# A four-layer graph network on one core: new item orders on all engines and new PSUM banks

## The reference

```python
x = LN(x + attention(x, adj))     # 8 heads; softmax/3 + adj/3 + exp(-adj)/3 as weights, W_out
x = LN(x + hypergraph(x, adj))    # h = LN(relu(Dn*(H B H^T x W1) + b1)); y = Dn*(H B H^T h W2) + b2 + x
x = LN(x + diffusion(x, adj))     # T = adj*exp(leaky(sj+si)) / row sum; relu(x Wk0 + T x Wk1 + T T x Wk2)
x = LN(x + mean_aggregate(x, adj))# relu([x, adj x / deg] W3)
```

## Time and profile before

| | us |
|---|---|
| median of 3 runs (lowest, highest) | 1391.9 (1388.77, 1392.45) |
| profiled execution, its own time | 1394.77 |
| span of the profiled execution | 1393.0 |
| PE busy | 1319.9 (95%) |
| PEld busy | 1132.3 (81%) |
| DVE busy | 1162.7 (83%) |
| ACT busy | 899.1 (65%) |
| POOL busy | 623.1 (45%) |
| TensorE's mean granted clock | 0.982 |

### The profile page before, as it was taken

One profiled execution on the slowest core, in us unless ns is written; L12 is line 12 of the kernel. 1 busy time (PEld: TensorE's weight loads), 2 busy tenths in 40 slices (PEclk: granted clock), 3 DMA queues, 4 the chain that ended last, 5 costly groups with the idle time before them and its releaser, 6 DMA issues.

```text
span 1393.0 us, 32474 instructions
## 1 busy us (share of the span) xinstructions
PE 1319.9 (95%) x9705; PEld 1132.3 (81%) x9705; DVE 1162.7 (83%) x3449; ACT 899.1 (65%) x2677; POOL 623.1 (45%) x1094
## 2 busy tenths in 40 slices
PE   4799999999999999999999999999999999999975
PEld 4688888888888888888888888888888888888863
DVE  2588888888888889888888888888988888888873
ACT  3466666667666666766666766666676666676641
POOL 3135444345554345545434454443554543445442
PEclk8899999999999999999999999999999999999996
DMA  5000000000000000000000000000000000000000
GB/s 186 14 14 21 20 11 16 12 20 20 20 11 16 12 20 20 20 20 11 16 12 20 20 20 19 12 13 15 20 20 20 11 16 12 20 20 20 9 8 8
DMA packets 35588, 28.32 MB, mean 20 GB/s; under 512 B 7664, under 2 KB 34416, under 8 KB 35568
## 3 DMA queue, kind: packets, MB, share of 16 engines
q1 hardware_dynamic: 33984, 27.27, 6.2%
q0 software_dynamic: 176, 0.52, 0.2%
q10 hardware_dynamic: 1408, 0.27, 0.1%
HBM read 19.67 MB, written 8.39 MB: 20 GB/s over the span
## 4 chain that ended last, share of the span: by engine, by line
issue 35%; POOL 24%; DVE 20%; PE 13%; ACT 2%; POOLq 1%; DVEq 1%; ACTq 0%
POOL rs L1441 9%; DVE prob L1124 7%; POOL rs L1439 4%; POOL resid L1478 3%; POOL resid L1480 3%; PE PS L405 3%; DVE neg_max L1115 3%; PE PS L401 2%; PE PS L402 2%; POOL xout L1496 2%; PE PS L526 2%; ACT yT_hi L914 2%; POOL gate L1464 2%; POOL yT_lo L1509 1%; DVE xT_lo L1057 1%
## 5 line engine op out<-in xcount | busy, mean ns | idle before, releaser
L1439 POOL TENSOR_TENSOR rs<-mv,eps_c 128x1 f32<-128x1 f32 (+1 forms) x288 | 60.2, 209 | 343.8 <-DVE mv L1065 343.7
L1124 DVE SCALAR_TENSOR_TENSOR prob<-prob,rl,gate 128x128 f32<-128x128 f32 x512 | 199.7, 450 | 6.6 <-DVE rl L1121 0.4
L833 ACT ACTIVATE prob<-PS,neg_max 128x128 f32<-128x128 f32 x512 | 180.1, 381 | 3.0 <-DVE neg_max L1115 1.8
L1441 POOL TENSOR_TENSOR rs<-rs,mhalf 128x1 f32<-128x1 f32 (+1 forms) x288 | 165.5, 575 | 22.6
L816 ACT ACTIVATE qk<-PS 128x512 f32<-128x512 f32 x128 | 76.5, 599 | 120.5 <-PE PS L479 120.4
L475 PE MATMUL PS<-xT_hi,wqk_hi 128*128 128x256 f32 x512 | 137.9, 290 | 6.4 <-DVE wk_lo L1050 4.3
L476 PE MATMUL PS<-xT_hi,wqk_lo 128*128 128x256 f32 x512 | 134.2, 284 | 0.0
L1505 POOL TENSOR_TENSOR z<-z,bk_bc 128x256 f32<-128x256 f32 x64 | 48.7, 780 | 188.5 <-ACT z L892 188.5
L833 ACT ACTIVATION_READ_ACCUMULATOR prob<-PS,neg_max 128x1 f32 x512 | 113.0, 221 | 0.0
L475 PEld LDWEIGHTS PS<-xT_hi,wqk_hi 128*128 128x128 f32 x512 | 98.4, 192 | 13.9 <-issue 11.5
L479 PE MATMUL PS<-xT_lo,wqk_hi 128*128 128x256 f32 x512 | 103.1, 283 | 0.0
(11 more groups left out here) (215 smaller groups left out, 4383.7 us busy)
## 6 DMA issues: line engine op xcount, KB each, us to landing
xin<-in_x_dram SPq DMA_DIRECT2D x32, 256.0 KB, 2.7
out_dram<-xout SPq DMA_DIRECT2D x32, 256.0 KB, 2.2
...
```

The costliest lines, as they stand in the source:

```text
L833: last = act.activation(prob[:, t, h, :], PS[:, bank, k * P:(k + 1) * P], ACT.Exp, bias=neg_max[:, t, h:h + 1], accum_out=row_sum[:, t, h: ...
L1124: last = dve.scalar_tensor_tensor(prob[:, t, h, :], prob[:, t, h, :], rl[:, t, h:h + 1], gate[:, t], ALU.mult, ALU.add)
L1439: step.done(pool.tensor_tensor(rs[:, n, gs, 0], mv[:, n, gs, 1], eps_c[:].to_broadcast([P, graphs]), ALU.add))
L1441: return pool.tensor_tensor(rs[:, n, gs, 1], rs[:, n, gs, 0], mhalf[:].to_broadcast([P, graphs]), ALU.pow)
```

## The change

The orders of the items in `group` are new on TensorE, ACT, DVE and POOL. All but a few PSUM banks are new, and with them the places where an `after` holds an item back. In the set-up, the first transposes and projections of group 0 on TensorE (`xT0_(0)`, `adjT_(0)`, `qk_(0, 0)`, `qk_(0, 1)`), which were a call of `group`, are written out in a fixed order with a wait behind each. No operation is added or taken away.

The banks of the table, three of its lines:

```diff
-        bank_qk = (4, 5, 3, 6)
+        bank_qk = (1, 1, 3, 6)
...
-        bank_si = (3, 4)
+        bank_si = (3, 3)
...
-        bank_T2 = (3, 1)
+        bank_T2 = (5, 6)
```

TensorE, the set-up and the group:

```diff
-                group(None, None, 0)
-
+                xT0_(0)
+                pe.wait_ge(act_xT0, 1)
+                pe.wait_ge(dve_xT0, 1)
+                adjT_(0)
                 pe.wait_ge(act_adjT, 1)
+                qk_(0, 0)
+                pe.wait_ge(act_qk, 1)
+                qk_(0, 1)
                 pe.wait_ge(act_qk, 2)
-                pe.wait_ge(dve_xT0, 1)
                 pe.wait_ge(set_beta, 2)
...
                 if F:
                     qk_(i, 2)
                 if B:
+                    after(pe, dve_o3, 2, s - 2, 1)
                     h_(j, 0)
                     h_(j, 1)
                 if F:
@@ -669,14 +674,19 @@
                     S_(i, 0)
                 if B:
                     hw_(j, 0)
+                    after(pe, dve_hT, 2, s - 1, 2)
                     hw_(j, 1)
                     y1_(j, 0)
+                if F:
+                    D_(i)
+                if B:
                     y1_(j, 1)
                 if F:
+                    S_(i, 1)
+                    after(pe, dve_mv1, 2, s - 1, 1)
                     v_(i, 0)
-                    after(pe, dve_mv1, 2, s - 1, 1)
-                    S_(i, 1)
-                    D_(i)
+                    after(pe, act_exp, 4, s, 2)
+                    AT_(i)
                 if B:
                     xT2_(j)
                 if F:
@@ -685,53 +695,55 @@
                 if B:
                     Z_(j, 0)
                 if F:
+                    after(pe, act_AT, 1, s, 1)
                     PT_(i, 0)
                 if B:
                     after(pe, act_exp, 4, s, 4)
                     si_(j, 0)
-                    after(pe, act_v, 2, s, 2)
                     Z_(j, 1)
-                if F:
                     after(pe, act_E, 4, s - 1, 2)
-                    after(pe, act_exp, 4, s, 3)
-                    after(pe, act_exp, 4, s, 4)
-                    AT_(i)
-                if B:
                     si_(j, 1)
-                if F:
+                if L:
+                    after(pe, act_PT, 2, s, 1)
+                    xT0_(n)
+                if F:
+                    after(pe, act_Z2, 2, s - 1, 1)
+                    after(pe, dve_Z2, 2, s - 1, 1)
+                    PT_(i, 1)
+                    after(pe, dve_Z2, 2, s - 1, 2)
+                    after(pe, act_Z2, 2, s - 1, 2)
                     PV_(i, 0)
-                if L:
-                    xT0_(n)
-                if F:
-                    after(pe, act_E, 4, s - 1, 4)
-                    PT_(i, 1)
                 if B:
                     T1_(j, 0)
                     T1_(j, 1)
-                if F:
-                    W_(i, 0)
+                if L:
+                    qk_(n, 0)
+                if F:
+                    after(pe, dve_Y, 2, s - 1, 1)
                     PV_(i, 1)
                 if B:
                     T2_(j, 0)
                     T2_(j, 1)
                 if L:
-                    qk_(n, 0)
+                    after(pe, act_qk, 4, s + 1, 1)
                     qk_(n, 1)
                 if F:
+                    W_(i, 0)
+                    after(pe, dve_o2, 2, s - 1, 1)
                     W_(i, 1)
                 if B:
                     xT3_(j, 0)
+                    xT3_(j, 1)
                 if L:
                     adjT_(n)
                 if B:
-                    after(pe, act_qk, 4, s + 1, 2)
-                    xT3_(j, 1)
                     Z3_(j, 0)
                     Z3_(j, 1)
+                if F:
+                    ax_(i, 0)
+                if B:
                     T3_(j, 0)
                 if F:
-                    ax_(i, 0)
-                    after(pe, act_qk, 4, s + 1, 1)
                     ax_(i, 1)
                 if B:
                     T3_(j, 1)
```

ACT (the end of its group), DVE and POOL (the parts that matter below):

```diff
                     v_(i, 1)
                 if B:
+                    Z01_(j, 0)
+                    E_(j, 0)
+                if F:
+                    PT_(i, 0)
+                if B:
                     Z2_(j, 0)
-                    E_(j, 0)
-                if F:
-                    PT_(i, 0)
-                if B:
-                    Z01_(j, 0)
-                    Z01_(j, 1)
+                    Z2_(j, 1)
                     E_(j, 1)
-                    Z2_(j, 1)
-                if F:
-                    AT_(i)
+                if L:
+                    xT0_(n)
                 if B:
                     al_(j, 0)
                     al_(j, 1)
-                if F:
+                    Z01_(j, 1)
+                if F:
+                    PT_(i, 1)
                     OT_(i, 0)
-                    carry(i)
-                    PT_(i, 1)
-                if L:
-                    xT0_(n)
                 if B:
                     Y_(j, 0)
                     Y_(j, 1)
-                if F:
+                if L:
+                    qk_(n, 0)
+                if F:
+                    carry(i)
                     OT_(i, 1)
                 if L:
-                    qk_(n, 0)
                     qk_(n, 1)
                 if B:
                     xT3_(j, 0)
                     xT3_(j, 1)
+                    Z3_(j, 0)
                 if L:
                     adjT_(n)
                 if B:
-                    Z3_(j, 0)
                     Z3_(j, 1)
                 if F:
+                    ax_(i, 0)
+                    ax_(i, 1)
                     x1_(i, 0)
                     x1_(i, 1)
-                    ax_(i, 0)
-                    ax_(i, 1)
 
             set_up()
             set_up_done(act)
...
-                if F:
                     counts()
                 if B:
                     y1_(0)
                     y1_(1)
+                if F:
+                    max_(1)
+                if B:
                     x2_(0)
                     x2_(1)
                 if F:
-                    max_(1)
                     norm_(0, 0)
                 if B:
                     xT2_()
                 if F:
+                    norm_(0, 1)
                     dcol_()
-                    norm_(0, 1)
                 if B:
                     Z_(0)
                 if F:
                     norm_(1, 0)
-                if B:
+                    norm_(1, 1)
+                if B:
+                    Z_(1)
+                    z2_(0)
                     gmax_(0)
-                if F:
-                    Dn_()
-                if B:
-                    Z_(1)
+                    z2_(1)
+                    gmax_(1)
                     al_(0)
-                if F:
-                    norm_(1, 1)
-                if B:
-                    gmax_(1)
                     al_(1)
-                    z2_(0)
                     all_(0)
-                    z2_(1)
                     all_(1)
-                if F:
-                    fOT_(0)
+                if L:
+                    front(n)[1]()
                 if B:
                     den_(0)
                     den_(1)
                     Y_(0)
                     Y_(1)
+                if F:
+                    Dn_()
+                if B:
                     Yl_()
-                if L:
-                    front(n)[1]()
-                if F:
-                    y0_(0)
+                if F:
+                    fOT_(0)
                 if B:
                     o2_(0)
                     o2_(1)
...
-                    resid_(0)
+                if F:
+                    gate_()
+                if B:
                     rsh_(0)
                     rsh_(1)
-                if F:
-                    gate_()
-                if B:
+                    resid_(0)
                     resid_(1)
+                if F:
+                    operator()
+                if B:
                     rs1_(0)
                     rs1_(1)
                 if F:
-                    operator()
                     fresid_()
                 if B:
                     z0_(0)
                     z0_(1)
```

More of the change, by code:

```diff
@@ L185, in gnn_stack_kernel @@
         bA, bB, bD, bC, bE, bP, bQ, bR = range(8)
-        bank_adjT = 6
+        bank_adjT = 0
         bank_xT0 = 2
-        bank_qk = (4, 5, 3, 6)
-        bank_D = 2
+        bank_qk = (1, 1, 3, 6)
+        bank_D = 0
         bank_v = (6, 6)
-        bank_AT = 3
-        bank_S = (0, 3)
-        bank_PT = (1, 4)
-        bank_PV = (1, 6)
-        bank_y0 = (0, 7)
-        bank_ax = (0, 4)
-        bank_h = (2, 1)
-        bank_hT = (4, 2)
-        bank_y1 = (3, 7)
-        bank_xT2 = 7
-        bank_Z01 = (5, 7)
-        bank_Z2 = (0, 6)
-        bank_si = (3, 4)
-        bank_T1 = (3, 7)
-        bank_T2 = (3, 1)
-        bank_xT3 = (3, 5)
-        bank_Z3 = (2, 7)
-        bank_T3 = (1, 6)
-        bank_hw = (6, 4)
+        bank_AT = 1
+        bank_S = (1, 3)
```

(54 more changed lines are left out.)

8 lines of the change are left out of this document (2 added, 6 removed).

## The result

The changed kernel takes 1388.56 us (median of 20 runs, 1386.14 to 1390.49); the kernel before, run beside it on the same chip, takes 1394.13 us (20 runs, 1388.77 to 1396.15). The ratio is 0.9962 with a 95% interval of 0.9954 to 0.9970: faster, by 5.6 us. The forecast was 24 us. The sign is right, the size is a quarter, and the time is where rival B had put it. The profiled execution took 1386.9 us.

A forecast was written before the change was run, and what follows sets the result against it. The prediction took TensorE, busy 95%, as the bound: 1.66 us of waits away and 0.80 new, net 0.86 a pass over 31 passes, 26.7 less, plus 2.4 for the set-up: 1367.6 us, own range 1355 to 1383.

The forecast's parts named there:

- rival B: The waits only move round the ring of four engines; new waits 1.5 to 1.7 a pass, 1388 to 1395 us; chance 0.14.
- The waits that go: TensorE waits at `Z_(j,0)`, `PT_(i,1)`, `T1_`, `y1_`, `T2_` and `xT3_` go: 1.66 us a pass.
- `x2`: the step that failed: At `xT2_`, later `x2` is level with TensorE's new cover: priced at nothing, up to 0.4 in the range.
- The prediction's own sign: Wrong if passes are over 40.8 apart; the largest TensorE distance names the place: `x2` at `xT2_`, POOL at `xT3_`.
- POOL's price: POOL operations beside DVE operations reading two SBUF tensors delay DVE 0.4 each; one such delay between `Y_` and `xT3_`.
- `T2_` (forecast 0.15 new, 0.2 away): At `T2_`, the old wait of 0.2 goes; about 0.15 comes because its last matmul reads DVE's delayed `yT_lo`.
- `xT3_` (forecast 0.25 new): At `xT3_`, DVE's path of 7.33 plus one POOL delay, 7.73, exceeds TensorE's cover of 7.5: new stall 0.25.
- `si_(j,1)` (forecast 0.2 new): `si_(j,1)` loses `AT_` as cover and waits for DVE's `sji` right behind `Z_(j,1)`: 0.2 a pass.
- The changes of kind: Two more switches on TensorE between fp32 transposes or products and three-part matmuls, 0.1 each: 0.2 a pass.
- The set-up: `qk_(0,1)` waits for the copy of `qk_(0,0)`, so the `gamma` product and everything behind shifts by 2.4 us, 1.3 to 3.
- A: Only TensorE's own work is left; all 1.66 go, only 0.2 comes: 1349 us; chance 0.18.
- C: Slower: POOL holds three DVE operations between `Y_` and `xT3_`, TensorE stalls 2.1 there: 1425 us; chance 0.14.

The follow-up runs named there:

- experiment 1: Changed kernel with POOL's sum of input and output bias held back until both `x2` are written: 1391.8 us, ratio 0.9988 to the kernel before.
- experiment 8: Kernel before, with only POOL's sum of input and output bias moved a pass ahead, to the end of the pass: 1378.5 us, ratio 0.9898.
- experiments 4 and 5: Changed kernel with POOL's sum of input and output bias cut to 8 of 256 columns: 1366.4 us; or whole, moved a pass ahead: 1366.6 us.
- experiment 7: Changed kernel with POOL's sum a pass ahead, `Dn_` behind `x1_(1)`, `Yl_` right behind `Y_`, and `xT0_(n)` ahead of `si_(j,1)`: 1379.6 us, ratio 0.9897.
- Experiment 6: Changed kernel with DVE's `Dn_` moved behind `x1_(1)` and `Yl_` right behind `Y_`: 1379.6 us, ratio 0.9901 to the kernel before.
- experiments 1 and 2: Changed kernel: first, POOL's sum held back until `x2` is done, 1391.8 us; second, DVE's `Yl_` put ahead of `Dn_`, 1398.8 us.
- experiment 9: Changed kernel, POOL's sum a pass ahead, `xT0_(n)` ahead of `si_(j,1)`, `Yl_` behind `Y_`, `Dn_` between `mv0_(1)` and `x1_(0)`: 1350.05 us, ratio 0.9689.

## Why the prediction was wrong in size

- **The waits that go (forecast 1.66 a pass).** What went is more than that: `Z_(j,0)` 0.54 for 0.43, `PT_` 0.21 and 0.14 for 0.3, `T1_` 0.58 for 0.33, `y1_` 0.14 for 0.2, `v_(i,0)` 0.17, not forecast, and 0.07 at `si_` and 0.09 at `W_`. That is 1.9. Of the forecast's terms the 0.2 at `xT3_` did not come (0.86 and 0.86), nor the 0.2 at `T2_`. At `Z_(j,0)` the order does what was told, since in experiment 1 the item is 2.12 although the sum stands beside `prob` again; but the prediction took that wait for DVE's order, and experiment 8 shows that it was POOL's.
- **`x2`: the step that failed.** The prediction said "By my count these two are level, so I price it at nothing, and at up to 0.4 in the range". It measured 1.0 (0.89 at `AT_` and 0.11 at `xT2_`). The miss of a pass is 0.86 less 0.26, so 0.6: this one term is more than the whole of it. With the sum out of the way `AT_` holds 0.72 (experiments 4 and 5) and `xT2_` 0.52: 0.27 and 0.11 are the order's, within the 0.4 allowed, and 0.62 is POOL's, for which there was no term. The prediction's own sign named the place ("at `xT2_` it is `x2`"). A new price of POOL was put only between `Y_` and `xT3_`, although the kernel before had the same sum beside other operations of DVE, where experiment 8 finds its price.
- **POOL's price.** The forecast took 0.4 for each meeting, from a mean over operations under way. An operation that starts with POOL's is held for nearly all of it: `x2` 0.8, `yT_lo` 0.54, `Dn` 1.0 in experiment 7. The Trainium skill (SBUF — State Buffer, "Who interferes with whom") says that whoever comes second is fully blocked for the other's instruction, and it counts `tensor_scalar`, in a two-port mode, among what can be blocked. The prediction told only the half on two inputs, and set its price aside. The runs agree with both halves: `x2`, a `tensor_scalar` with one tensor and two columns of 128x1, took 1.35 for 0.38. No run here shows which mode it ran in.
- **`T2_` (forecast 0.15 new, 0.2 away).** The place and the neighbour were right, the size was not: `T2_` went from 0.90 to 1.19, 0.29 more. Experiment 6 shows 0.82 with `yT_lo` free, so the block cost 0.37, and only 0.08 of the 0.2 was there to be won.
- **`xT3_` (forecast 0.25 new).** It did not come. DVE's path from `yv` to `x3` is 712.75 to 719.31, 6.56 with the block in it, where 6.33 and one delay of 0.4 were forecast; TensorE waited for it at `T2_` first, and so had the time at `xT3_`. An operation that reads PSUM was undisturbed, as told: `oT_lo`, at 715.09 beside POOL's `aT_lo`, took 0.68.
- **`si_(j,1)` (forecast 0.2 new).** Measured 0.27 at `Z_(j,1)` less 0.07 at `si_`: right, with `sji` behind four `prob` of 1.42 beside POOL's `z`.
- **The changes of kind (forecast 0.2 new).** The four `qk_` of a pass took 0.09 more, `T3_` and `ax_` together 0.01. With these the items' medians give 1.9 away and 1.65 new, 0.3 less, where the pass has 0.26.
- **The set-up (forecast 2.4).** 2.0: right in size, partly by luck. The `gamma` product started 1.4 later than forecast, and at the higher granted clock it was 1.76 shorter, which the forecast had not counted on.
- **The rivals.** B had the time (1388 to 1395), and its general reason, that a wait taken away shows up in the next place, is what experiments 1 and 2 show. Its own terms were wrong: `x2` 0.4 for 1.0, `xT3_` 0.6 for nothing, ACT 0.3 to 0.5 for nothing found. A's time was reached only by experiment 9, with POOL's work placed by what it runs beside. C, the three blocks on the way to `xT3_`, did not happen: only one of them met POOL.
- **The range.** Its upper end of 1383 isn't what its own terms add up to: 0.4 at `x2` and 0.35 more at `xT3_`, 31 times, with 0.6 of the set-up and 2 of the ends, reach 1393. So the terms at their worst allowed for the measured 1388.6, though the stated 1383 did not.
